# A two-layer metaformer block on one core: the load of x by tokens moved behind the spectral loads, ScalarE's copies ahead of the next part, and a narrower subtraction of the taps

## The chip, the core and the metric

The kernel runs on one core of a Trainium2 chip. The metric is the device time of one execution in microseconds (us). Five engines work side by side: TensorE (PE; its weight loads are listed as PEld), VectorE (DVE), ScalarE (ACT), GpSimd (POOL) and SyncE (SP), which here issues all data transfers. They meet only at semaphores: an instruction waits until a counter has reached a value, and its engine executes in program order, so everything behind a waiting instruction waits as well.

## The reference

The input x is 8 x 64 x 64 x 64 (batch, channels, height, width). Every step is a residual one:

```
x = x + spectral_conv(layernorm_channels(x))      # 32 x 32 kept modes, kernel looked up by f1^2 + f2^2
t = tokens(x);  t = t + moe(layernorm(t))         # 8 experts of 64 x 64, the best 2 of a softmax router
x = x + depthwise_conv_29x29(layernorm_channels(x))
t = tokens(x);  t = t + moe(layernorm(t))
```

## The kernel before, in words

**Stages.** The x that is held in SBUF has three layouts in turn. `xr` (x by rows) and `xb` (x by channels) are loaded first, in pieces; VectorE measures the layer norm's statistics on `xr` and TensorE takes the first Fourier transform from `xb`. `xr` lies in the region `X`. Once it has been measured, the same region takes x by tokens (`x_tok`, four transfers of 2 MB), onto which the result of the spectral convolution is added much later. The order of the work is written out by hand in every engine's program.

**The spectral product.** 136 complex matrices of 64 x 64 are read in eight blocks of 17 (`t` = 0 to 7, from `spec_pairs`). SyncE loads block `t` into one of three buffers; for `t` of 3 and more it first waits until VectorE has split block `t - 3` (`k_low`). ScalarE (`row_high`, L1172) takes the high half of each block, VectorE (`row_low`, L747) the low half, and TensorE multiplies (L1492, about 1000 small matmuls, straight-line code without a loop). Then follow transposes (L1558), the inverse transforms (L1570 and L1707), and VectorE adds the result to X (L1069), which waits for `x_tok`.

**SyncE's order before.** In the loop over the blocks, at `t` = 2, it waits until all of `xr` has been measured (`piece_measured`) and then issues the four transfers of `x_tok`; the loads of blocks 3 to 7 and the weights of the experts come behind them in the same queue.

**The expert stage.** It runs once for each layer, over 8 chunks of 32 token tiles. A chunk has 16 pairs `p`. For pair `p` TensorE multiplies two tiles with seven experts (L1605, L1606: `expert_pair`), VectorE multiplies the result with the gates (L904: `weigh_pair`), GpSimd adds the products (L571, L581), and TensorE sums four tiles in PSUM every second pair (L1616, L1619: `sum_quad`).

Beside it the same engines prepare the chunks ahead, in parts `(k, j)` of 8 tiles, four to a chunk. Each part goes through a chain of five steps:

1. ScalarE: `normalise` (8 activations, L1249, cut in two halves of 4) and `take_high` (L1261), which writes the high half in f16
2. VectorE: `low_parts` (L844), the low half. The next part's `normalise` waits for it, since both use one PSUM bank
3. TensorE: `turn_tokens` (L1583), 8 transposes into another single bank, which must have been copied out before
4. ScalarE: `copy_parts` (L1278, L1279), the copy out of that bank
5. TensorE: `route` (L1593, L1594), the router's logits; VectorE then computes the gates in 15 small steps (L866 to L892)

The first chunk of each layer is `start_chunk`, whose order stands in tables. At pair `p` ScalarE starts the first half of `normalise` by `START_NORMS = {1: (1, 2), 3: (1, 3), 5: (2, 0), 8: (2, 1), 12: (2, 2)}`, does the second half one pair later, and copies by `START_TURNS = {0: (1, 0), 3: (1, 1), 5: (1, 2), 7: (1, 3), 9: (2, 0), 13: (2, 1)}`. A first half and a copy fall on the same pair at 3 and at 5 only. TensorE turns by the same table, behind its `expert_pair(p)`; VectorE does `low_parts` at pairs 1, 3, 5, 7, 10 and 14.

**The taps.** The 29 x 29 taps of the depthwise convolution are split into high and low f16 halves within the first layer's start chunk: `taps_high` on ScalarE at pair 10 (L1316), `taps_low` on VectorE at pair 13 (L950). Both run over all 2412 columns of a padded row, in which the taps of a channel fill 29 rows of 29 at a pitch of 38; the rest is zero. `taps_low` works on partitions 64 to 127 only.

Of the kernel before, what the change touches and what calls it, by code (L numbers as in the profile page):

```python
# [15 lines left out]
B, C, H, W = 8, 64, 64, 64  # L16
# [6 lines left out]
NT = HB * WB * B  # L23
BO, BP, B2 = 2, 2, 2
BH, BQ = 2, 4
KS = 29
NE = 8
KRING = 3
PITCH = 38
# [4 lines left out]
CENTRE = 31 * PITCH + 23  # L34
TAP_SCALE = 256.0
# [32 lines left out]
def metaformer(nc, x_chan, x_rows, x_tok, spec_pairs, spec_last, dft, dft16, inv_h, inv_c, ident, ident16,  # L68
               experts0, experts1, rank, taps, out):
    ctx = ExitStack()  # L70
    with ctx:
# [11 lines left out]
        X = sb("X", NT * C)  # L83
# [63 lines left out]
        taps_f32 = R1[:, 5120:5120 + TAPS]  # L147
# [21 lines left out]
        x_in = sem("x_in")  # L169
# [189 lines left out]
        @block.sync  # L359
        def _(sp):  # L360
            def piece(i):
                return slice(i * PC, (i + 1) * PC)

            def unit(i):
                piece, g0, g1 = UNITS[i]
                return slice(piece * PC + g0 * C, piece * PC + g1 * C)

            def load_rows(i):
                sp.dma_start(X[:, unit(i)], x_rows[:, unit(i)]).then_inc(xr_in[i], 16)

            def load_channels(i):
                sp.dma_start(xb[:, unit(i)], x_chan[:, unit(i)]).then_inc(xb_in[i], 16)

            load_rows(0)
            sp.dma_start(dft_sb[:, :], dft).then_inc(dft_in, 16)
            sp.dma_start(rank_sb[:, :], rank).then_inc(rank_in, 16)
            load_channels(0)
            load_rows(1)
            load_channels(1)
            load_rows(2)  # L380
            load_rows(3)
            load_channels(2)
            load_rows(4)
            load_channels(3)
            load_channels(4)
            load_rows(5)
            load_channels(5)
            sp.dma_start(dft16_sb[:, :], dft16).then_inc(const_in, 16)
            lo, hi = BLOCKS

            for r, i in ((lo, 0), (hi, 1)):
                sp.dma_start(last_raw[r, 0:17, 0:64], spec_last[:, i]).then_inc(last_in, 16)
                sp.dma_start(last_raw[r, 0:17, 64:128], spec_last[:, 1 - i]).then_inc(last_in, 16)

                sp.dma_start(last_raw[r, 17, 0:64], spec_last[:, 1 - i, 16]).then_inc(last_in, 16)
                sp.dma_start(last_raw[r, 17, 64:128], spec_last[:, i, 16]).then_inc(last_in, 16)
            sp.dma_start(inv_h_sb[:, 0:64], inv_h).then_inc(const_in, 16)
            sp.dma_start(inv_c_sb[:, :], inv_c).then_inc(const_in, 16)
            sp.dma_start(ident_sb[:, :], ident).then_inc(const_in, 16)
            sp.dma_start(ident16_sb[:, :], ident16).then_inc(const_in, 16)  # L400
            for t in range(NSTEP):
                if t < 3:
                    sp.wait_ge(c_dft, 20 + 2 * t)
                else:
                    sp.wait_ge(k_low, 2 * (t - 2))
                for r in BLOCKS:
                    sp.dma_start(k_raw[t % 3][r], spec_pairs[:, PER_STEP * t:PER_STEP * t + PER_STEP, :]
                                 ).then_inc(k_in[t % 3], 16)
                if t == 2:

                    sp.wait_ge(piece_measured, len(UNITS))
                    for i in range(4):
                        n = NT * C // 4
                        sp.dma_start(X[:, i * n:(i + 1) * n], x_tok[:, i * n:(i + 1) * n]).then_inc(x_in, 16)

            wait_c_dft_low(sp, 32)
            sp.dma_start(raws_at[0], experts0).then_inc(raw_in, 16)

            sp.wait_ge(inv2, 32)
            for r in BLOCKS:  # L420
                sp.dma_start(taps_f32[r], taps).then_inc(taps_in, 16)
            sp.wait_ge(taps_step, TAPS_STEPS)
            for p in range(P):
                at = (WI - 1 - p // HI) * PITCH + HI - 1 - p % HI
                sp.wait_ge(y_used, 12 + 17 * p // 20)
                sp.dma_start(taps_dram[:, :, p, :].rearrange("s c n -> (s c) n"),
                             taps_16[:, at:at + WINDOW]).then_inc(taps_out, 16)
            sp.wait_ge(taps_out, P * 16)

            def load_bands(c, i):  # L430
                src = bass.AP(taps_dram[:, :, :, :].tensor, c * P * WINDOW,
                              [[WINDOW, P], [C * P * WINDOW, 2], [1, WINDOW]])
                sp.dma_start(bands[i], src).then_inc(bands_in[i], 16)

            sp.wait_ge(summed, NOCT * (NCHUNK - 1))
            load_bands(0, 0)
            sp.wait_ge(summed, NOCT * NCHUNK)
            for i in range(1, 4):
                load_bands(i, i)
            sp.dma_start(raws_at[1], experts1).then_inc(raw_in, 16)  # L440
            with sp.Fori(0, C // 4 - 1) as m:
                for i in range(4):
                    sp.wait_ge(blocks_ready, 4 * m + i + 1)
                    sp.wait_ge(low_blocks_ready, 4 * m + i + 1)
                    load_bands(4 * m + 4 + i, i)
            sp.wait_ge(conv_copied, C)

            def store(tile, tiles):
                at = slice(tile * C, (tile + tiles) * C)
                sp.dma_start(out[:, at], X[:, at]).then_inc(stored, 16)  # L450

            for i in range(2 * NCHUNK - 1):
                sp.wait_ge(sum_copied, NOCT * NCHUNK + (i + 1) * NOCT // 2)
                store(i * CT // 2, CT // 2)
            sp.wait_ge(sum_copied, 2 * NOCT * NCHUNK - 1)
            store(NT - 16, 8)
            sp.wait_ge(last_copied, 2)
            store(NT - 8, 4)
            sp.wait_ge(sum_copied, 2 * NOCT * NCHUNK)
            store(NT - 4, 4)  # L460
            sp.wait_ge(stored, (2 * NCHUNK + 2) * 16)
# [195 lines left out]
        def _(dve):  # L657
# [288 lines left out]
            def taps_low():  # L946

                dve.wait_ge(taps_step, 1)
                r = BLOCKS[1]
                dve.scalar_tensor_tensor(out=taps_16[r], in0=taps_f32[r], scalar=TAP_SCALE, in1=taps_16[r],  # L950
                                         op0=ALU.mult, op1=ALU.subtract).then_inc(taps_step, 1)

            def plane_stats(lo, hi):
# [167 lines left out]
        def _(act):  # L1121
# [117 lines left out]
            def normalise(layer, k, q, j, tiles=range(8)):  # L1239

                n = layer * NCHUNK + k
                if 0 in tiles:
                    if j == 0:
                        act.wait_ge(tok_step, (n + 1) * TOK_STEPS)
                    if layer or j or k:
                        act.wait_ge(tok_low, n * 4 + j)
                for t in tiles:
                    at = 8 * j + t
                    last = act.activation(xn_psum[:, t * C:(t + 1) * C], X[:, bass.ds(k * CT * C + at * C, C)],  # L1249
                                          ACT.Identity, bias=small[2 * q][:, at:at + 1],  # L1250
                                          scale=small[2 * q + 1][:, at:at + 1])
                if 7 not in tiles:
                    return
                last.then_inc(tok_normed, 1)
                if layer or k:
                    act.wait_ge(across, n * 4 + j - 3)
                act.wait_ge(tok_normed, n * 4 + j + 1 - 4 * layer)
                take_high(j, xn_psum)
# [59 lines left out]
            def start_chunk(layer):  # L1318
                for p in range(NPAIR):
                    if p % 4 == COPY_AT and p >= 4 * SUM_LAG:  # L1320
                        copy_sum(layer, 0, p // 4 - SUM_LAG)
                    if p in START_NORMS:
                        k, j = START_NORMS[p]
                        normalise(layer, k, k % 2, j, range(0, 4))
                    if p - 1 in START_NORMS:
                        k, j = START_NORMS[p - 1]
                        normalise(layer, k, k % 2, j, range(4, 8))
                    if p in START_TURNS:
                        k, j = START_TURNS[p]
                        copy_parts(layer, k, k % 2, j)  # L1330
                    if p == 2:
                        root_seed(layer, 2, 0)
                    if not layer and p == 10:
                        taps_high()
                    if p == START_EXP:
                        exp_second(layer, 1)
                    if p == ROOT_AT:
                        root_seed(layer, 3, 1)
# [453 lines left out]
```

## Time and profile before

| | us |
|---|---|
| median of 3 runs (lowest, highest) | 957.55 (956.13, 961.07) |
| the profiled execution | 955.84 |
| its span | 954.1 |
| VectorE busy in the span | 774.4 |
| GpSimd busy in the span | 567.5 |
| ScalarE busy in the span | 506.9 |

The page gives TensorE as busy for 850.6 us, with a mean granted clock of 0.936 of full speed. The stretches of the span are: Fourier transforms to 82 us, spectral product to 115 us, inverse transforms to 186 us, first expert stage to about 449 us, depthwise convolution to about 684 us, second expert stage to the end. The chain that ended last passes from engine to engine; what is taken from it shortens the span, as long as no other wait takes its place.

### The profile page before, as it was taken

The page shows a single profiled execution, that of the slowest core. Times are in us where ns is not written, and L with a number is a line of the kernel's source. Part 1 is how long each engine was busy: PE and PEld are TensorE (multiplying, and loading weights), DVE is VectorE, ACT ScalarE, POOL GpSimd, SP SyncE. Part 2 cuts the span into 40 slices and gives each one's busy share as a digit, 9 for nine tenths or more (in the row PEclk, how much of TensorE's full clock was granted, in tenths as well). Part 3 has the DMA queues.
Part 4 walks back from the last instruction along what each step waited for, and adds up shares of the span by engine and source line. Part 5 has one row for each costly group of instructions (what it writes and reads, how often), then busy time and mean ns, then how long its engine had stood idle before and what let it go on. Part 6 is the DMA issues. An engine that isn't in the chain of part 4 may idle for free.

```text
span 954.1 us, 24392 instructions
## 1 busy us (share of the span) xinstructions
PE 850.6 (89%) x9482; PEld 699.1 (73%) x9482; DVE 774.4 (81%) x1421; ACT 506.9 (53%) x1051; POOL 567.5 (59%) x504
## 2 busy tenths in 40 slices
PE   6997888677999998996899999999658999999998
PEld 6996877645676666654899999999635666667665
DVE  5768698888999989999787677774787999998884
ACT  2467485786667766211444444444168676676511
POOL 3780203157798887796654334330216888889888
PEclk9997577988999999999899999999959999999999
DMA  9997100103777776683787877888000010101101
GB/s 377 355 294 258 50 1 2 40 15 153 281 311 300 301 300 274 280 323 122 265 282 253 286 264 259 274 275 264 13 1 13 33 46 24 45 24 45 46 40 49
DMA packets 48291, 163.09 MB, mean 171 GB/s; under 512 B 9424, under 2 KB 9936, under 8 KB 46032
## 3 DMA queue, kind: packets, MB, share of 16 engines
q1 hardware_dynamic: 48208, 161.96, 46.7%
q8 instruction: 55, 0.90, 0.4%
q14 instruction: 28, 0.23, 0.1%
HBM read 93.46 MB, written 68.49 MB: 170 GB/s over the span
## 4 chain that ended last, share of the span: by engine, by line
PE 50%; DVE 31%; POOL 6%; issue 5%; DMA 3%; ACT 3%; SPq 1%; POOLq 0%; DVEq 0%; ACTq 0%
PE pair L1692 23%; DVE R L904 11%; PE pair L1619 5%; PE pair L1605 5%; PE pair L1606 4%; DMA X<-x_rows 3%; PE pair L1616 3%; DVE R L844 3%; PE pair L1492 3%; POOL R L571 3%; DVE R L660 2%; PE pair L1583 2%; DVE R L833 2%; DVE work L660 2%; ACT pair L1249 1%
## 5 line engine op out<-in xcount | busy, mean ns | idle before, releaser
L904 DVE TENSOR_TENSOR R<-pair,R 128x896 f32<-128x896 f32 x256 | 275.1, 1082 | 41.8 <-PE pair L1606 40.6
L571 POOL TENSOR_TENSOR R<-R 128x768 f32<-128x768 f32 x128 | 231.9, 1812 | 85.8 <-DVE R L904 76.7
L1692 PE MATMUL pair<-R 128*128 (+4 forms) x2880 | 226.8, 242 | 9.8 <-DVE R L982 9.2
L1692 PEld LDWEIGHTS pair<-R 128*128 128x128 f16 x2880 | 223.9, 98 | 12.9 <-issue 10.5
L1249 ACT ACTIVATE pair<-X,work 128x64 f32<-128x64 f32 x480 | 166.7, 394 | 97.1 <-DVE R L844 94.6
L1605 PE MATMUL pair<-work,R 128*128 128x448 f16 x512 | 185.0, 361 | 22.4 <-DVE R L904 20.9
L1606 PE MATMUL pair<-work,R 128*128 128x448 f16 x512 | 184.4, 360 | 0.0
L581 POOL TENSOR_TENSOR R<-R 128x512 f32<-128x512 f32 x128 | 164.9, 1288 | 10.0
L997 DVE COPY R<-R 128x1152 f32<-128x1152 f32 x64 | 93.1, 1455 | 64.9 <-PE pair L1692 64.3
L1367 ACT COPY R<-R 128x1152 f32<-128x1152 f32 x64 | 81.9, 1282 | 117.4 <-PE pair L1692 117.4
L1619 PE MATMUL pair<-R,ident_sb 128*128 128x256 f32 x496 | 128.4, 381 | 0.0
L623 POOL TENSOR_TENSOR R<-X,work 128x1024 f32<-128x1024 f32 x15 | 43.9, 2929 | 103.5 <-DVE R L988 90.4
L1605 PEld LDWEIGHTS pair<-work,R 128*128 128x128 f16 x512 | 50.7, 99 | 73.7 <-DVE R L904 42.3
L1619 PEld LDWEIGHTS pair<-R,ident_sb 128*128 128x128 f32 x496 | 95.0, 191 | 13.1
L660 DVE BATCH_NORM_STATS2 work<-X 128x6 f32<-128x128 f32 x384 | 84.9, 282 | 14.4 <-DMA X<-x_rows 14.4
L1616 PE MATMUL pair<-X,inv_h_sb 128*128 128x256 f32 x248 | 79.7, 403 | 0.0
L1291 ACT ACTIVATE X<-pair 128x512 f32<-128x512 f32 x62 | 36.0, 580 | 73.8 <-PE pair L1625 73.8
L1606 PEld LDWEIGHTS pair<-work,R 128*128 128x128 f16 x512 | 50.9, 99 | 30.7 <-issue 2.0
L1583 PE MATMUL pair<-ident_sb,R 128*128 128x128 f16 x512 | 42.9, 232 | 33.9 <-DVE R L844 27.1
L1583 PEld LDWEIGHTS pair<-ident_sb,R 128*128 128x128 f16 x512 | 36.1, 104 | 48.2 <-DVE R L844 30.4
L1453 PE MATMUL pair<-dft_sb,R 128*128 128x68 f32 x256 | 56.1, 422 | 9.1 <-DMA R<-x_chan 9.1
L1453 PEld LDWEIGHTS pair<-dft_sb,R 128*128 128x128 f32 x256 | 55.2, 333 | 9.3 <-issue 8.9
(137 smaller groups left out, 1292.7 us busy)
## 6 DMA issues: line engine op xcount, KB each, us to landing
taps_halves<-R SPq DMA_DIRECT2D x128, 458.5 KB, 3.3
R<-taps_halves SPq DMA_DIRECT2D x64, 917.0 KB, 4.8
X<-x_tok SPq DMA_DIRECT2D x4, 2048.0 KB, 17.8
out<-X SPq DMA_DIRECT2D x15, 512.0 KB, 2.6
R<-spec_pairs SPq DMA_DIRECT2D x16, 272.0 KB, 5.4
X<-x_rows SPq DMA_DIRECT2D x4, 1024.0 KB, 10.6
R<-x_chan SPq DMA_DIRECT2D x4, 1024.0 KB, 13.7
X<-x_rows SPq DMA_DIRECT2D x2, 2048.0 KB, 27.3
```

The source lines that it names most:

```text
L571: pool.tensor_tensor(pr[:, :, 192:384], pr[:, :, 0:192], pr[:, :, 192:384], ALU.add).then_inc(half_ready, 1)
L581: pool.tensor_tensor(w, pr[:, :, 192:320], pr[:, :, 320:448], ALU.add).then_inc(quarter_ready, 1)
L660: return dve.bn_stats(out_.rearrange("p t k -> p (t k)"), rows.rearrange("p t c -> p c t"))
L904: dve.tensor_tensor(pr.rearrange("p t (e c) -> p t e c", c=C), pair[p % 2][:, :].rearrange("p (t e c) -> p t e c", t=2, c=C)[:, :, 0:NE - ...
L1249: last = act.activation(xn_psum[:, t * C:(t + 1) * C], X[:, bass.ds(k * CT * C + at * C, C)], ACT.Identity, bias=small[2 * q][:, at:at + 1 ...
L1453: mm = pe.matmul(c_dft_bank(n)[:, j * 68:(j + 1) * 68], xb[:, (4 * n + j) * P:(4 * n + j + 1) * P], dft_sb[:, :], start=True, stop=True)
L1583: mm = pe.transpose(out_[:, t * P:(t + 1) * P], parts[j][:, t * P:(t + 1) * P], ident16_sb[:, :])
L1605: pe.matmul(dst, u[q][:, t * P:(t + 1) * P], wa[:, 0:EW], start=True, stop=False)
L1606: mm = pe.matmul(dst, vh[q][:, t * P:(t + 1) * P], wb[:, 0:EW], start=False, stop=True)
L1616: pe.matmul(bank[7][:, 256 * half:256 * (half + 1)], ident_scaled, X[:, bass.ds((k * NQUAD + g) * 256, 256)], start=True, stop=False)
L1619: pe.matmul(bank[7][:, 256 * half:256 * (half + 1)], ident_sb[:, :], w[:, :, j, :], start=False, stop=False)
L1692: mm = pe.matmul(acc[:, y0:y1, x0:x1, :], blocks[i % 2][:, ks, 2 - y, 1 - x, :], src[:, y0 + y:y1 + y, x0 + x:x1 + x, :], start=(ks == 0 a ...
```

## The change

SyncE issues `x_tok` behind all eight blocks and behind the first layer's expert weights. In the start chunk of both layers ScalarE does `copy_parts` ahead of the first half of `normalise` where both fall on one pair. `taps_low` runs over the 29 rows of 29 columns that hold taps.

```diff
@@ block.sync
                     sp.dma_start(k_raw[t % 3][r], spec_pairs[:, PER_STEP * t:PER_STEP * t + PER_STEP, :]
                                  ).then_inc(k_in[t % 3], 16)
-                if t == 2:
-
-                    sp.wait_ge(piece_measured, len(UNITS))
-                    for i in range(4):
-                        n = NT * C // 4
-                        sp.dma_start(X[:, i * n:(i + 1) * n], x_tok[:, i * n:(i + 1) * n]).then_inc(x_in, 16)
 
             wait_c_dft_low(sp, 32)
             sp.dma_start(raws_at[0], experts0).then_inc(raw_in, 16)
+            sp.wait_ge(piece_measured, len(UNITS))
+            for i in range(4):
+                n = NT * C // 4
+                sp.dma_start(X[:, i * n:(i + 1) * n], x_tok[:, i * n:(i + 1) * n]).then_inc(x_in, 16)
@@ taps_low
-                dve.scalar_tensor_tensor(out=taps_16[r], in0=taps_f32[r], scalar=TAP_SCALE, in1=taps_16[r],
+                first = CENTRE - KS // 2 * (PITCH + 1)
+                f32, f16_ = (m[r, first:first + KS * PITCH].rearrange("p (x y) -> p x y", y=PITCH)[:, :, 0:KS]
+                             for m in (taps_f32, taps_16))
+                dve.scalar_tensor_tensor(out=f16_, in0=f32, scalar=TAP_SCALE, in1=f16_,
                                          op0=ALU.mult, op1=ALU.subtract).then_inc(taps_step, 1)
@@ start_chunk on ScalarE
-                    if p in START_NORMS:
-                        k, j = START_NORMS[p]
-                        normalise(layer, k, k % 2, j, range(0, 4))
                     if p - 1 in START_NORMS:
                         k, j = START_NORMS[p - 1]
                         normalise(layer, k, k % 2, j, range(4, 8))
                     if p in START_TURNS:
                         k, j = START_TURNS[p]
                         copy_parts(layer, k, k % 2, j)
+                    if p in START_NORMS:
+                        k, j = START_NORMS[p]
+                        normalise(layer, k, k % 2, j, range(0, 4))
```

## Rows read from the trace of the kernel before

**Rows 1.** The page's part 4: the chain that ended last, by engine.

```profile
PE 50%; DVE 31%; POOL 6%; issue 5%; DMA 3%; ACT 3%; SPq 1%; POOLq 0%; DVEq 0%; ACTq 0%
```

**Rows 2.** Timeline, PE, spectral product: start, us, engine, line, operation, count, idle before.

```profile
82.50 3.88 PE L1492 MATMUL pair<-R 128*128 128x16 f16 x143 [1.50 <-DVE R L729]
89.23 3.56 PE L1492 MATMUL pair<-R 128*128 128x16 f16 x128 [2.85 <-issue]
92.96 3.56 PE L1492 MATMUL pair<-R 128*128 128x16 f16 x128 [0.18 <-issue]
96.97 3.58 PE L1492 MATMUL pair<-R 128*128 128x16 f16 x128 [0.44 <-issue]
101.25 13.49 PE L1492 MATMUL pair<-R 128*128 128x16 f16 x487 [0.70 <-issue]
```

**Rows 3.** DMA queues from 72.7 to 74.5 us: packets, MB, share.

```profile
q8 instruction: 1, 0.02, 3.8%
```

**Rows 4.** DMA queues from 82.6 to 86.4 us, the only queue listed.

```profile
q1 hardware_dynamic: 213, 0.72, 86.5%
```

**Rows 5.** DMA queues from 86.4 to 88 us.

```profile
q8 instruction: 1, 0.02, 5.0%
```

**Rows 6.** Windows: stretch, us, busy by engine, PE clock, DMA share, GB/s.

```profile
60.00:80.00 20.00, 15.81 (x199) 14.99 (x197) 15.58 (x26) 14.96 (x26) 8.23 (x12) 1.00 1.02 413
231.00:237.70 6.70, 4.56 (x47) 3.49 (x48) 5.29 (x12) 3.95 (x10) 4.52 (x4) 0.50 0.99 385
```

**Rows 7.** Timeline of SP's queue, 0 to 220 us: DMA issues.

```profile
56.40 2.02 SPq L414 DMA_DIRECT2D X<-x_tok  x4
...
74.55 21.36 SPq L407 DMA_DIRECT2D R<-spec_pairs  x10
```

**Rows 8.** Timeline of all engines: VectorE's first addition to X.

```profile
151.68 0.69 DVE L1069 TENSOR_TENSOR X<-X,pair 128x512 f32<-128x512 f32 x1 [1.63 <-PE pair L1707]
```

**Rows 9.** Timeline of ACT, start chunk of the first layer.

```profile
201.75 1.40 ACT L1249 ACTIVATE pair<-X,work 128x64 f32<-128x64 f32 x4
203.09 0.57 ACT L1278 COPY R<-pair 128x512 f32<-128x512 f32 x1
...
206.93 1.40 ACT L1249 ACTIVATE pair<-X,work 128x64 f32<-128x64 f32 x4 [0.82 <-DVE R L844]
...
210.72 0.59 ACT L1261 CAST R<-pair 128x512 f16<-128x512 f32 x1
```

**Rows 10.** Timeline of PE, the same chunk: the transposes of part (1, 2).

```profile
204.28 0.61 PE L1583 MATMUL pair<-ident_sb,R 128*128 128x128 f16 x8 [2.35 <-ACT R L1279]
```

**Rows 11.** Timeline of DVE, first layer: pairs 6 and 10, taps, last gate, pair 2.

```profile
207.70 1.09 DVE L904 TENSOR_TENSOR R<-pair,R 128x896 f32<-128x896 f32 x1 [0.46 <-PE pair L1606]
...
216.86 1.09 DVE L904 TENSOR_TENSOR R<-pair,R 128x896 f32<-128x896 f32 x1 [0.70 <-PE pair L1606]
...
224.75 3.59 DVE L950 SCALAR_TENSOR_TENSOR R<-R 64x2412 f16<-64x2412 f32 x1
...
232.61 0.39 DVE L892 TENSOR_TENSOR R<-R,pair 128x224 f32<-128x224 f32 x1
...
239.61 1.09 DVE L904 TENSOR_TENSOR R<-pair,R 128x896 f32<-128x896 f32 x1 [2.47 <-PE pair L1606]
```

**Rows 12.** Timeline of ACT, start chunk of the second layer.

```profile
718.56 1.40 ACT L1249 ACTIVATE pair<-X,work 128x64 f32<-128x64 f32 x4
```

**Rows 13.** Timeline of PE, start chunk of the second layer: part (1, 2).

```profile
721.09 0.61 PE L1583 MATMUL pair<-ident_sb,R 128*128 128x128 f16 x8 [3.36 <-ACT R L1279]
```

**Rows 14.** Timeline of DVE, second layer: pairs 6 and 10, last gate, pair 2.

```profile
726.17 1.09 DVE L904 TENSOR_TENSOR R<-pair,R 128x896 f32<-128x896 f32 x1 [2.13 <-PE pair L1606]
...
734.12 1.09 DVE L904 TENSOR_TENSOR R<-pair,R 128x896 f32<-128x896 f32 x1 [0.70 <-PE pair L1606]
...
746.13 0.39 DVE L892 TENSOR_TENSOR R<-R,pair 128x224 f32<-128x224 f32 x1
...
751.23 1.09 DVE L904 TENSOR_TENSOR R<-pair,R 128x896 f32<-128x896 f32 x1 [1.34 <-PE pair L1606]
```

## The prediction

> **What bounds the kernel now.** I read the chain that ended last first. It is half TensorE and a third VectorE, with ScalarE and GpSimd together under a tenth [rows 1], so no engine is the limit throughout, and each edit must be weighed where it acts. I then read the timelines of three stretches: the spectral product, where the chain is TensorE's matmuls, and the start chunk of each expert stage, where it wanders between ScalarE, TensorE and VectorE. The last 50 us are GpSimd's additions, but these start when VectorE delivers, so what is gained earlier shifts them as a whole.
>
> **x by tokens behind the blocks.** The edit adds and removes nothing; it moves four transfers of 2 MB past ten block loads and one load of expert weights. Before, they are issued at 56.4 us and fill the DMA engines from 60 to 80 us at 413 GB/s [rows 6, 7]. The block loads that wait behind them could make ScalarE late, but ScalarE's split of block 3 must wait for TensorE's block 0 anyway, and the wait for the load that is left is 0.6 us and not on the chain. So the order of data is worth nothing here.
>
> What I do see is TensorE's idle time for "issue". The matmuls of L1492 come in groups: 143, then three times 128, then 487, with gaps of 2.85, 0.18, 0.44 and 0.70 us ahead of the later four [rows 2]. Each matmul has one weight load, so the groups are 256 instructions long, and the queue named "instruction" moves packets of 0.02 MB. I read the gaps as TensorE waiting for its own code. Going back 128 matmuls from the gap at 86.4 us, the block of code before it was entered at 82.9 us. The packet that should have started then is missing from 82.6 to 86.4 us, while other traffic holds 86.5% of the engines [rows 4], and appears behind 86.4 us [rows 5]. It came late because block 3, held up by `x_tok`, and block 4 then move together. Without `x_tok` ahead of it block 3 is in by 79 us, and only block 4 is in the way. The later groups met one such load each, at gaps of 0.18 to 0.70 us. I take 0.5 us for the gap: a gain of 2.85 - 0.5 = 2.3 us, bounds 0 (the gap stays) and 2.85 (it goes).
>
> Against this stands the new place. The block loads end at 95.9 us [rows 7], a little earlier then, and the expert weights follow; `x_tok` moves its 8 MB from about 95 to 115 us, by the 20 us that it takes now [rows 6]. TensorE enters four or five blocks of code in that time. How does a fetch fare beside `x_tok`? One row shows it: a block entered at 73.0 us got its packet within the stretch to 74.5 us [rows 3], in the middle of the full load. A group of 487 matmuls in 13.49 us without a gap [rows 2] is 27.7 ns each, or 3.55 us for a block, and the fetches just keep pace. I charge 0.1 us for each of five: 0.5 us. Bounds: nothing, and 5 times the 2.35 us by which the first gap exceeds an ordinary one, 12 us. I take the low end, since the row at 73 us is the one under this very load. X is not needed before 151.7 us [rows 8], 35 us behind its arrival, so nobody waits for it; if that cover were gone, VectorE's additions would wait. GpSimd's own wait for `x_in` moves from a time when it idles to another. This edit: 2.3 - 0.5 = 1.8 us gained, bounds -12 and +2.9.
>
> The Trainium skill (Runtime: NRT & Kernel Launch, Instruction fetch mechanics) says that code is streamed in blocks of 256 instructions, one being fetched while the other executes, and that crossing into a new block is mostly hidden. The block length agrees with the groups of 128 matmuls and 128 loads; that it is hidden does not agree with the gaps of 0.18 to 2.85 us [rows 2]. By that rule the gap would have another cause, this edit would be worth nothing, and the sum below would be 8.8 us instead of 10.6.
>
> **Copies ahead of the next part.** This acts at pairs 3 and 5 of both start chunks. First layer, pair 3: ScalarE is free at 201.7 us, runs four activations to 203.1 us, and only then copies part (1, 1), which TensorE had turned by 200.4 us [rows 9]. TensorE stands for 2.35 us until this copy's end before it turns part (1, 2) [rows 10]. With the copy first, 0.57 and 0.57 us overlapping to 1.0, TensorE goes on at 202.8 instead of 204.3 us. The total of ScalarE's work up to `take_high` of (1, 3) is the same, so VectorE's low half of it does not come later (206.2 us). Pair 5: ScalarE idles 0.82 us for that low half and then normalises from 206.93 us [rows 9]. With the copy of (1, 2) first, turned by 203.5 us now, 1.0 us of copying fills the idle time; `normalise` starts at 207.0, and `take_high` of (2, 0) moves from 210.7 to 209.75 us.
>
> Followed through: VectorE's pair 6 moves from 207.7 to 207.2 (TensorE no longer late), its low half of (2, 0) from 211.3 to 210.35, pair 8 from 212.9 to 211.4, pair 9 to 212.8, the two first gate steps to 214.65. TensorE can turn (2, 0) once (1, 3) is copied at 211.2, and has pair 10 ready 2.6 to 3.3 us later, at most 214.6. Pair 10 starts at 214.7 instead of 216.86 us [rows 11]: 2.15 us. From there VectorE has no idle time to the end of the chunk, and the gain stays.
>
> Second layer: TensorE waits 3.36 us for the same copy [rows 13], ScalarE starts with the activations at 718.56 us [rows 12], and pair 6 comes at 726.17 us with 2.13 us of idle time for TensorE [rows 14]. With the copy first, TensorE turns at 719.7, pair 6 is ready at 723.0 and VectorE takes it at 724.0, behind its low half (unchanged at 722.95). `take_high` of (2, 0) is done at 727.2 instead of 728.1, pair 8 goes from 730.15 to 728.25, TensorE turns (2, 0) at 728.35 behind the copy of (1, 3), and pair 10 starts at 731.7 instead of 734.12 [rows 14]: 2.4 us. Both: 4.55 us. Bounds: a loss of 1.0 us for each pair and layer, if the copies only postpone the chain of `normalise` (-4), and a gain of both of TensorE's waits, 2.35 + 3.36 = 5.7 us.
>
> **The taps.** 29 x 29 = 841 elements instead of 2412. At the rate of the row, 3.59 us / 2412 = 1.49 ns each [rows 11], that is 1.25 us: 2.34 us less on VectorE, which runs without idle time from pair 10 to the last gate. `taps_high` is ready long before. Pairs 14 and 15 are waiting from TensorE. Bounds: 0 if a strided row costs as much as the full one, 3.1 us if only a small fixed part is left.
>
> **The clock behind the taps.** While VectorE works on the taps TensorE has nothing to do, and from 231.0 to 237.7 us its granted clock is 0.50, the 1.2 GHz level [rows 6]. Just there it is late: pair 2 of the next chunk comes at 239.61 us after 2.47 us of idle time [rows 11]. From the end of the last gate step (233.0) to pair 2 it is 6.6 us. In the second layer, with no taps and at full clock, the same way takes 751.23 - 746.52 = 4.7 us [rows 14]. With the taps shorter TensorE's stop before is about 0.6 instead of 2.9 us, as in the second layer, and I expect its clock to stay up: 1.9 us, bounds 0 and 2.5 (the whole idle time).
>
> **Sum.** 1.8 + 4.55 + 2.34 + 1.9 = 10.6 us. The profiled execution took 955.84 us and lies 1.7 us under the median of the runs, 957.55. 957.55 - 10.6 = 947.0 us.
>
> **The rivals.**
> - *The code fetch and the clock give nothing.* The first gap has another cause or block 4 alone holds the packet up as long, and the clock drops as before, since TensorE also idles 2.7 us for the last gate. For it: a single block load already makes gaps up to 0.70 us. Against it: the second layer. Left are 4.55 + 2.34: 950.7 us.
> - *The copies gain half.* VectorE's low half of (1, 3) is not earlier by either order, and at pair 8 another wait (GpSimd's sums for the four product buffers) may come up. For it: the chain is short of slack everywhere. Against it: GpSimd idles 1.4 to 2 us ahead of each addition here. Left are 2.3 + 2.34 and one of the other two terms: 951.0 to 952.9 us, say 952.
> - *Slower: the code fetch starves beside `x_tok`.* Place: the spectral product from 95 to 115 us, where TensorE runs through a block of code in 3.55 us and is itself the chain. Price: if each of five fetches comes late as the one at 82.9 us did, 5 x 2.65 = 13 us; if none is served until the 20 us of transfer are over, about 18 us. For it: the packet that is missing for 3.6 us in rows 4. Against it: rows 3. Then it is 957.55 - 11.1 + 13 = 959.5, or up to 965 us. It turns the sum above 2.2 us a fetch.
> - *The first edit does nothing and the rest works* lies within the range of the forecast, at 948.8 us.
>
> **How the numbers follow.** Forecast, with 944 to 950 us as its own range: 0.52. First rival 0.18, second 0.14, slower rival 0.07, and 0.09 for more than I sum up (stretches at the lower clock may fall at other places once the stages start earlier, and where TensorE is the chain that is worth 1 to 2 us either way). A measurement of this kernel can tell 0.5% (4.8 us) from no change, so faster means below 952.8 us. That holds for the forecast, the first rival, most of the second and the better case: 0.79. Within 0.5%: 0.15, slower 0.06. The range from 942 to 955 us leaves out the slower rival and tails.
>
> **What would show it.** In the profile after: the gap ahead of the second group of L1492 under 1 us, and no gap over 0.5 us from 95 to 115 us; TensorE's wait for L1279 ahead of part (1, 2) shorter by 1.4 us in both layers, and pair 10 earlier by about 2 us against the stage's start; L950 at 1.25 us; a clock of 1.0 throughout the first 15 us of the first layer's second chunk. The prediction is wrong if gaps named "issue" of 2 us stand in the spectral product, or if `normalise` of (2, 0) comes later than before.

## The result, and the profile after

The changed kernel takes 961.39 us (median of 20 runs, 959.64 to 962.69) against 957.33 us (20 runs, 954.24 to 961.07): ratio 1.0039, 95% interval 1.0031 to 1.0048. It is slower by 4 us where 10 us less were forecast. The profiled execution took 961.60 us, with a span of 959.8. Of all runs below one stands apart, 2939.71 us among the 12 of the copies alone, and its ratio leaves it out.

I lay the starts of VectorE's 256 `weigh_pair` beside each other, after minus before. They show where the time comes and goes:

| place | before, us | after minus before, us |
|---|---|---|
| first layer, pair 0 | 194.87 | +8.50 |
| pair 6 | 207.70 | +7.81 |
| pair 10 | 216.86 | +7.35 |
| pair 14 (behind the taps) | 228.37 | +5.70 |
| next chunk, pair 2 | 239.61 | +5.93 |
| second layer, pair 0 | 710.12 | +5.86 |
| pair 6 | 726.17 | +3.49 |
| pair 10 | 734.12 | +4.24 |
| next chunk, pair 2 | 751.23 | +5.74 |

So 8.5 us are lost ahead of the expert stage. The first layer's start chunk gains 1.15 us by the copies (pair 0 to pair 10) and 1.65 us by the taps (pair 10 to pair 14), the second layer's 1.6 us by the copies; and 0.2 and 1.5 us go again behind the two start chunks.

The loss stands in TensorE's timeline of the spectral product (start, us, line, count, idle before), which answers to [rows 2]:

```profile
82.26 3.90 PE L1493 MATMUL pair<-R 128*128 128x16 f16 x143 [1.70 <-DVE R L727]
87.06 3.56 PE L1493 MATMUL pair<-R 128*128 128x16 f16 x128 [0.89 <-issue]
91.07 3.56 PE L1493 MATMUL pair<-R 128*128 128x16 f16 x128 [0.45 <-issue]
96.44 3.58 PE L1493 MATMUL pair<-R 128*128 128x16 f16 x128 [1.81 <-issue]
102.64 3.79 PE L1493 MATMUL pair<-R 128*128 128x16 f16 x128 [2.62 <-issue]
109.12 3.79 PE L1493 MATMUL pair<-R 64*64 64x16 f16 x128 [2.69 <-issue]
115.60 3.58 PE L1493 MATMUL pair<-R 128*128 128x16 f16 x128 [2.69 <-issue]
120.98 2.91 PE L1493 MATMUL pair<-R 128*128 128x16 f16 x103 [1.80 <-issue]
```

Now every group of 128 matmuls has a gap before it, and the gaps sum to 12.95 us instead of 4.17. The first shrank from 2.85 to 0.89 us; where `x_tok` moves, the last four are 1.8 to 2.7 us wide. The clock does not tell the two kernels apart here: in every stretch of 4 us from 84 us to the end of the product it is 0.50 to 0.52, the 1.2 GHz level, in both. SyncE's queue, which answers to [rows 7], and one window of the stretch (as in [rows 6]: clock, DMA share, GB/s at the end):

```profile
95.21 2.28 SPq L415 DMA_DIRECT2D X<-x_tok  x4
```

```profile
104.00:108.00 4.00, 2.43 (x91) 2.33 (x87) 2.57 (x2) 1.49 (x2) 0.00 (x0) 0.50 1.00 422
```

The block of code that TensorE entered at 102.64 us has its fetch missing from 103 to 106.6 us, while data holds the DMA engines, and present right behind:

```profile
q1 hardware_dynamic: 110, 1.54, 100.6%
```

```profile
q1 hardware_dynamic: 36, 0.59, 100.7%
q8 instruction: 1, 0.02, 4.8%
```

This is the same picture as in [rows 4, 5], once for each block of code. The start chunk, VectorE's timeline after, answers to [rows 11]: pairs 6 and 10, the taps, pair 2 of the next chunk.

```profile
215.51 1.07 DVE L902 TENSOR_TENSOR R<-pair,R 128x896 f32<-128x896 f32 x1
...
224.21 1.09 DVE L902 TENSOR_TENSOR R<-pair,R 128x896 f32<-128x896 f32 x1 [1.19 <-PE pair L1607]
...
232.09 1.95 DVE L951 SCALAR_TENSOR_TENSOR R<-R 64x841 f16<-64x841 f32 x1
...
245.54 1.09 DVE L902 TENSOR_TENSOR R<-pair,R 128x896 f32<-128x896 f32 x1 [2.69 <-PE pair L1607]
```

TensorE's timeline, answering to [rows 10, 13]. Its wait for the copy fell from 2.35 to 0.36 us and from 3.36 to 1.87 us, but a new one stands five pairs later, for ScalarE's first copy of a sum:

```profile
211.31 0.61 PE L1584 MATMUL pair<-ident_sb,R 128*128 128x128 f16 x8 [0.36 <-ACT R L1280]
...
221.64 0.67 PE L1617 MATMUL pair<-X,inv_h_sb 128*128 128x256 f32 x2 [0.83 <-ACT X L1292]
...
725.47 0.61 PE L1584 MATMUL pair<-ident_sb,R 128*128 128x128 f16 x8 [1.87 <-ACT R L1280]
...
735.80 0.67 PE L1617 MATMUL pair<-X,inv_h_sb 128*128 128x256 f32 x2 [0.82 <-ACT X L1292]
```

Two windows of the kernel after at the lower clock: behind the first layer's start chunk, as before, and behind the second layer's, where it was at full clock before; pair 2 answers to the last of [rows 14].

```profile
237.10:243.90 6.80, 5.05 (x49) 3.83 (x50) 4.90 (x12) 3.55 (x9) 4.83 (x3) 0.50 1.00 382
...
752.50:755.90 3.40, 3.40 (x30) 2.68 (x28) 1.63 (x5) 1.06 (x2) 3.32 (x3) 0.50 0.00 0
```

```profile
756.97 1.09 DVE L902 TENSOR_TENSOR R<-pair,R 128x896 f32<-128x896 f32 x1 [2.84 <-PE pair L1607]
```

### The profile page after: what moved, and what is told of

Its sections match the earlier page's. It is cut to its first block, busy times and chain, and to the rows that moved or that the text cites. A ratio compares the mean times of both kernels' runs of the same rounds, so it can differ in the third digit from the quotient of the medians.

```text
span 959.8 us, 24392 instructions
## 1 busy us (share of the span) xinstructions
PE 850.5 (89%) x9482; PEld 698.0 (73%) x9482; DVE 771.9 (80%) x1421; ACT 506.1 (53%) x1051; POOL 566.4 (59%) x504
## 4 chain that ended last, share of the span: by engine, by line
PE 48%; DVE 30%; issue 7%; POOL 6%; ACT 5%; DMA 3%; SPq 1%; POOLq 0%; DVEq 0%; ACTq 0%
PE pair L1693 23%; DVE R L902 11%; PE pair L1620 5%; PE pair L1606 4%; PE pair L1607 4%; DMA X<-x_rows 3%; PE pair L1617 3%; PE pair L1493 3%; POOL R L569 3%; DVE R L842 3%; DVE R L658 2%; ACT pair L1250 2%; DVE work L658 2%; DVE R L831 2%; PE pair L1584 2%
## 5 line engine op out<-in xcount | busy, mean ns | idle before, releaser
L569 POOL TENSOR_TENSOR R<-R 128x768 f32<-128x768 f32 x128 | 231.9, 1812 | 85.1 <-DVE R L902 74.1
## 6 DMA issues: line engine op xcount, KB each, us to landing
X<-x_rows SPq DMA_DIRECT2D x4, 1024.0 KB, 11.2
```

What stands on the lines that cost most here:

```text
L569: pool.tensor_tensor(pr[:, :, 192:384], pr[:, :, 0:192], pr[:, :, 192:384], ALU.add).then_inc(half_ready, 1)
```

## The experiments

**x_tok alone behind the blocks** (the first hunk of the diff, nothing else).

> x_tok moved behind the blocks, nothing else changed. Theory 1 (TensorE's code fetches starve beside x_tok): gaps named issue of 2.6 to 2.7 us between groups of 128 matmuls as in the changed kernel, the first expert stage starts 8.5 us later than in the kernel before, and the time is 957.3 + 8 = 965 to 966 us. Theory 2 (the load in its new place is harmless, the loss of 4 us comes from the new orders of ScalarE and VectorE): 955 to 957.5 us, gaps under 1 us.

965.12 us against 958.05, ratio 1.0077 (1.0062 to 1.0092). TensorE's groups from 97 us on:

```profile
97.13 3.59 PE L1490 MATMUL pair<-R 128*128 128x16 f16 x128 [1.79 <-issue]
104.42 3.79 PE L1490 MATMUL pair<-R 128*128 128x16 f16 x128 [3.71 <-issue]
110.89 3.80 PE L1490 MATMUL pair<-R 64*64 64x16 f16 x128 [2.68 <-issue]
116.82 3.58 PE L1490 MATMUL pair<-R 128*128 128x16 f16 x128 [2.13 <-issue]
121.64 2.91 PE L1490 MATMUL pair<-R 128*128 128x16 f16 x103 [1.24 <-issue]
```

The whole loss, and more, is in this one edit: +7 us.

**The copies alone** (the third hunk).

> ScalarE's copies ahead of the first half of normalise, nothing else changed. Theory 1: pair 10 comes 1.2 us earlier in the first layer and 1.6 us earlier in the second, less than the 2.15 and 2.4 forecast, since TensorE now waits 0.8 us for ScalarE's first copy of a sum; 954.5 us if no stretch at the lower clock moves against it, 956 if one does as in the second layer of the changed kernel (1.5 us). Theory 2 (this order is the loss): 959 us or more.

956.25 us, ratio 0.9986 (0.9976 to 0.9996). TensorE waits 0.8 us for the copy of the first sum here too. Pair 10 gained 1.15 us and 1.6 us against the start of its stage, and 0.5 us went again behind the first start chunk and 1.6 us behind the second, where a stretch at the lower clock stands (747.5 to 750.7 us).

**The taps alone** (the second hunk).

> taps_low over 29 rows of 29 columns, nothing else changed. Theory 1: the instruction takes 1.95 us instead of 3.59 as in the changed kernel, and the time falls by 1.6 us to 955.7 us; the clock behind it still drops to 0.50. Theory 2 (TensorE's shorter stop keeps its clock up): 3.5 us less, 953.8 us.

956.26 us, ratio 0.9980 (0.9968 to 0.9991). The instruction took 1.95 us, and the clock behind it still fell, for 6.8 us. So the 1.65 us come in and the clock's 1.9 us don't. The profiled executions of these two kernels, which have `x_tok` at its old place, show gaps of 5.39 and 7.15 us in all in the spectral product, where that of the kernel before had 4.17: executions differ in this by some microseconds.

**x_tok behind the spectral product**, with both other edits.

```diff
             sp.wait_ge(piece_measured, len(UNITS))
+            sp.wait_ge(mixed, NMIX)
             for i in range(4):
```

> The changed kernel, but x_tok is issued only when TensorE has finished the whole spectral product, so that it moves from about 115 to 137 us beside the transposes and inverse transforms, where TensorE waits for VectorE anyway. Theory 1 (a transfer beside code that runs without a pause): the gaps of 2.6 us are gone, the first gap stays near the 0.9 us of the changed kernel, the product ends 1.5 to 2.5 us earlier than before, and the time is 957.3 - 2 - 2.8 = 952 to 954 us. Theory 2 (x_tok costs the same wherever its 20 us are put): 959 to 962 us.

952.43 us, ratio 0.9947 (0.9933 to 0.9960): 5 us faster than before and 9 us faster than the changed kernel, by one wait. TensorE's groups, as above:

```profile
87.04 3.56 PE L1494 MATMUL pair<-R 128*128 128x16 f16 x128 [0.79 <-issue]
91.33 3.56 PE L1494 MATMUL pair<-R 128*128 128x16 f16 x128 [0.72 <-issue]
95.88 3.58 PE L1494 MATMUL pair<-R 128*128 128x16 f16 x128 [0.99 <-issue]
100.16 11.05 PE L1494 MATMUL pair<-R 128*128 128x16 f16 x384 [0.70 <-issue]
111.37 2.92 PE L1494 MATMUL pair<-R 128*128 128x16 f16 x103 [0.15 <-issue]
```

The gaps sum to 3.35 us. The same 8 MB now move from 114 to 137 us at 366 GB/s beside the transposes and inverse transforms, and cost nothing that can be seen. TensorE's transposes behind the product, in the kernel before and in this one:

```profile
116.43 11.17 PE L1558 MATMUL pair<-ident_sb,R 128*102 128x128 f16 x136 [1.69 <-DVE R L811]
```

```profile
115.98 10.63 PE L1560 MATMUL pair<-ident_sb,R 128*102 128x128 f16 x136 [1.69 <-DVE R L810]
```

The fetch of code is late here too: its packet starts at 120.38 us, 6.1 us behind the end of the product, where in the kernel before it started at 117.61 us, 2.9 us behind it. But no gap named "issue" follows from 116 to 150 us. These transposes take 78 ns each, so a block of 128 of them lasts 10 us and not 3.56, and a fetch that comes 3 us late is still in time. So it is the length of the block that hides the fetch, and not TensorE's waiting for VectorE, as I had expected: within these transposes it waits for nobody. This is read from the two profiles; no run of its own tests it.

**Smaller rows.** The changed kernel with 16 transfers of 4 KB rows for 4 of 16 KB.

```diff
-            for i in range(4):
-                n = NT * C // 4
+            for i in range(16):
+                n = NT * C // 16
                 sp.dma_start(X[:, i * n:(i + 1) * n], x_tok[:, i * n:(i + 1) * n]).then_inc(x_in, 16)
```

> The changed kernel, with x_tok in 16 transfers of 512 KB (rows of 4 KB) in place of 4 of 2 MB (rows of 16 KB), at the same place. Theory 1a (a fetch of code waits for a number of packets that are queued ahead of it on its DMA engine, each of 16 KB and 0.61 us): smaller packets shorten the wait, the gaps of 2.7 us shrink to 1.0 us or less, and the time is 955 to 957 us. Theory 1b (it waits for its share of a loaded engine, whatever the packets): gaps of 2.7 us, 961 us.

961.04 us, ratio 1.0040 (1.0026 to 1.0053), with gaps of 3.17, 2.41, 2.41 and 2.62 us under the load. The size of the rows makes no difference; theory 1a has fallen. The Trainium skill (DMA: Bandwidth & Descriptors, Queues, rings and completion order) says that a DMA engine takes turns between queues packet by packet. By that rule packets a quarter as long should have made the wait for a turn shorter. The packets did become shorter (4 KB and 0.16 us each by their records, for 16 KB and 0.61 us), and this run does not agree: its wide gaps of 2.41 to 3.17 us are no narrower than the 1.80 to 2.69 us of the changed kernel.

**Half of x_tok behind the product** (two transfers at the new place, then `sp.wait_ge(mixed, NMIX)`, then two).

> The changed kernel, with two of the four transfers of x_tok behind the blocks and two behind the spectral product. Theory 1 (each fetch beside the transfer costs 2.7 us): the stretch under load is half as long, two of the four gaps of 2.7 us remain, and the time lies midway between the changed kernel and the one with x_tok behind the product: 956 to 957.5 us. Theory 2 (any piece of x_tok in the product makes the same delay, as through a single late load): 960 us or more.

957.01 us, ratio 0.9987 (0.9976 to 0.9999), midway between 961.4 and 952.4. Two of the wide gaps are left, 3.17 and 2.41 us, and then it runs on:

```profile
102.78 3.79 PE L1495 MATMUL pair<-R 128*128 128x16 f16 x128 [3.17 <-issue]
108.98 7.32 PE L1495 MATMUL pair<-R 64*64 64x16 f16 x256 [2.41 <-issue]
116.73 2.91 PE L1495 MATMUL pair<-R 128*128 128x16 f16 x103 [0.43 <-issue]
```

The price goes with the time under load: one late fetch for each block of code that is entered in it.

**Spare traffic in the kernel before.**

```diff
             sp.dma_start(raws_at[0], experts0).then_inc(raw_in, 16)
+            for i in range(4):
+                n = NT * C // 4
+                sp.dma_start(spare_dram[:, i * n:(i + 1) * n], x_tok[:, i * n:(i + 1) * n]).then_inc(spare_out, 16)
```

> The kernel before, with x_tok at its old place, and behind the expert weights four more transfers of 2 MB from the input to a spare DRAM region that nobody reads or waits for until the end. Theory 1 (traffic alone delays the fetches): gaps of 2 us and more between groups of 128 matmuls from 96 us on, and 963 to 967 us. Theory 2 (the loss comes from x_tok writing SBUF or from somebody waiting for it): no such gaps, 957 to 959 us.

970.73 us, ratio 1.0138 (1.0122 to 1.0154). Nobody reads this region, X is where it was, and the gaps are there: 1.52, 2.41, 3.23 and 3.45 us.

```profile
102.81 3.79 PE L1498 MATMUL pair<-R 128*128 128x16 f16 x128 [1.52 <-issue]
109.01 3.79 PE L1498 MATMUL pair<-R 64*64 64x16 f16 x128 [2.41 <-issue]
116.04 3.58 PE L1498 MATMUL pair<-R 128*128 128x16 f16 x128 [3.23 <-issue]
123.07 2.91 PE L1498 MATMUL pair<-R 128*128 128x16 f16 x103 [3.45 <-issue]
```

Traffic alone does it. It cost 13 us, more than expected: this kernel has both the late first gap of the kernel before (3.08 us) and the new ones, and the transfer to DRAM lasted to about 125 us instead of 118, at 307 to 344 GB/s from 108 us on instead of 430, so that the last block, too, met a fetch of full lateness (3.45 us instead of 1.80). Pair 0 comes 11.2 us later than in the kernel before; another 1.2 us goes at the lower clock behind the second start chunk.

**The copy of the first sum ahead of the next part.** `x_tok` behind the product, and in the start chunks:

```diff
+                    if p == 8:
+                        copy_sum(layer, 0, 0)
-                    if p % 4 == COPY_AT and p >= 4 * SUM_LAG:
+                    if p % 4 == COPY_AT and p > 4 * SUM_LAG + COPY_AT:
                         copy_sum(layer, 0, p // 4 - SUM_LAG)
```

> The changed kernel with x_tok behind the product, and in both start chunks ScalarE's first copy of a sum ahead of the first half of normalise at pair 8 in place of pair 9. Theory 1 (the reordered copies gain 1.0 and 0.8 us less than forecast because TensorE now waits 0.8 us in each layer for this copy): TensorE's wait for L1292's counterpart goes, pair 10 comes 0.5 to 0.8 us earlier in each layer, and the time is 951 to 952 us. Theory 2 (the low half of part (2, 0) sets pair 10, not TensorE): unchanged, 952.4 us.

949.68 us, ratio 0.9912 (0.9898 to 0.9926); a second measurement gave 950.03 us against 956.85, ratio 0.9932 (0.9910 to 0.9954).

> The kernel with x_tok behind the product and the sum copy at pair 8 once more, beside the one with taps_low behind pair 14, so that their difference of 0.9 us is read on one chip. Theory 1: 949 to 951 us and 0.9 us above the other. Theory 2: the same as the other.

In the first layer TensorE's `sum_quad` ahead of pair 10 no longer waits, and pair 10 gained 2.1 us against pair 0, as forecast for the change. A wait of 1.0 us for the second copy of a sum stands ahead of pair 14 instead; there VectorE has the taps to do, and pair 14 is not later for it. In the second layer the gain is 1.7 us in the first profiled execution, which fell back to the lower clock for 3.4 us within the start chunk (717.0 to 720.3 us), and 2.6 us in the second, which did not. Against the kernel without this edit (1.15 and 1.6 us) that is 1.0 us a layer where nothing disturbs it, and theory 1's mechanism holds. The size by the times is not settled: set against 0.9947 the two ratios give 3.4 and 1.4 us, and the second interval overlaps that of the kernel without the edit (0.9933 to 0.9960).

**The taps behind pair 14** (`p == 13` to `p == 14` for `taps_low`, on top of the last kernel).

> The kernel with x_tok behind the product and the sum copy at pair 8, with taps_low behind pair 14 in place of pair 13, where GpSimd runs only its small Newton steps. Theory 1 (taps_low stood 1.0 us of its 1.95 us behind GpSimd's addition of 1.81 us that had begun before it; its own 841 elements take 0.9 us): the instruction takes 0.9 to 1.1 us, GpSimd's addition behind it is back at 1.27 us, and the time falls by 0.9 us, to 948.8 us. Theory 2 (a strided row of 29 costs 2.3 ns an element wherever it runs): 1.95 us again, 949.7 us.

949.39 us against 950.03, ratio 0.9921 (0.9900 to 0.9941) beside 0.9932. The mechanism of theory 1 shows, its gain does not: the intervals overlap almost wholly. VectorE's timeline and GpSimd's small step beside it, which takes 0.24 us elsewhere:

```profile
223.49 1.09 DVE L903 TENSOR_TENSOR R<-pair,R 128x896 f32<-128x896 f32 x1 [0.66 <-PE pair L1610]
226.00 1.03 DVE L952 SCALAR_TENSOR_TENSOR R<-R 64x841 f16<-64x841 f32 x1
```

```profile
226.08 1.06 POOL L551 TENSOR_TENSOR work<-work,rank_sb 128x32 f32<-128x32 f32 x1
```

The taps take 1.03 us, and GpSimd's second addition, now ahead of them, is back at 1.27 us; but pair 14, reached earlier, waits 0.66 us for TensorE; at the next chunk the two kernels are 0.1 us apart.

## Why the prediction was wrong

**The code fetch: the mechanism was right, and the row that was to price it was misread.** The cause of the gaps was named correctly, and so was what would happen in the worst case: the rival that starves "beside `x_tok`" is what the chip did. The step that failed is "a block entered at 73.0 us got its packet within the stretch to 74.5 us", from which I charged 0.1 us a fetch. The packet in [rows 3] is real; the 73.0 us was not read but counted back over some 13 us of timeline, through instructions and records whose number is not exact. The kernel after shows the error. There TensorE has the same code up to this place and the same pace (its groups of L1471 start at 70.25 and 72.48 us, those of the kernel before at 70.49 and 72.72), and from 70.5 to 72.4 us, with no `x_tok` moving, its queue has

```profile
q8 instruction: 1, 0.02, 3.5%
```

Its packet starts at 71.3 us by the packet's own record, that of the kernel before at 73.9. So the block was entered before 71.3 us, and the fetch beside `x_tok` was 2.4 us late, 2.64 less the 0.24 us by which TensorE is ahead in the kernel after. The other profiles agree: the packet starts at 73.9 to 74.1 us in the four kernels with `x_tok` at its old place, and at 71.2 to 72.0 us in the eight profiles of the others. No gap followed there because TensorE, waiting for VectorE, did not reach the next block before about 82.9 us, by the count in the prediction. The row that I took as evidence for harmlessness showed the price: the 2.35 us of my upper bound. I had both figures in the same text and took the low end by the row "under this very load". The last four gaps of the kernel after sum to 9.80 us; the same four blocks have 0.85 us with `x_tok` behind the product, and 1.95 to 2.22 us in the three profiles of the later kernels with that order. All gaps together are 8.8 us more than in the kernel before, and pair 0 comes 8.5 us later.

The spare traffic shows that the load alone suffices, the half transfer that it goes by the time under load, and the wait on `mixed` that the same late fetch costs nothing beside the transposes, where a block of code lasts 10 us. The Trainium skill (Runtime: NRT & Kernel Launch, Instruction fetch mechanics) calls the crossing mostly hidden; in the profiled executions here it is not: even with `x_tok` behind the product gaps of 0.15 to 2.07 us stand ahead of most of its blocks.

**The first gap: right.** Forecast 2.3 us less, measured 1.96 less (2.85 to 0.89), and 0.75 to 1.11 us in the other kernels without `x_tok` ahead of block 3, against 2.45 to 3.28 us with it.

**The copies: right in direction, about half in size.** Forecast 4.55 us, measured 2.8. TensorE did go on earlier, pair 6 came as computed (0.7 us earlier against pair 0 instead of 0.5; 2.4 in the second layer instead of 2.2), and so did pair 8. I then followed `normalise` and `turn_tokens` up to pair 10 but left out ScalarE's `copy_sum`, which stands at pair 9 behind the first half of `normalise` (2, 1), and for which `sum_quad` at pair 10 waits. With pair 10 reached earlier it became the last: 1.15 instead of 2.15 us, 1.6 instead of 2.4. Put one pair earlier, it gives the first layer's forecast value.

**The taps: the term was mis-sized.** Forecast 1.25 us for 841 elements at 1.49 ns, measured 1.95. The rate was taken from a row in which VectorE had stood still. In the kernel before, GpSimd's addition of 1.81 us began at 224.00 us and ended at 225.81; the taps "start" at 224.75 and end at 228.34, which is 225.81 plus 2412 elements at 1.05 ns. In the kernel after GpSimd's addition runs from 231.34 to 233.14 us, and the taps end at 234.04: 0.9 us, or 1.07 ns an element, behind it. The waiting is the same in both; what falls away is 1571 elements at 1.05 ns, 1.65 us (measured 1.64). GpSimd's next addition, held up from its usual 1.27 to 3.57 us before, takes 1.94 us after. The Trainium skill (SBUF — State Buffer, Who interferes with whom) says that a VectorE instruction with two inputs in SBUF and a GpSimd instruction that reads SBUF exclude each other for their whole length, whichever began first winning. Both directions agree with these rows, and so does the run with the taps at pair 14 (1.03 us).

**The clock behind the taps: wrong.** I blamed TensorE's stop of 2.94 us during the taps. With the stop shortened to 1.22 us (0.6 had been forecast) the clock fell to 1.2 GHz at the same place for 6.8 us, in the kernel after and with the taps alone; pair 2 waited 2.69 us. In three of the later profiles it fell for 3.4 us there, one of them with a stop of only 0.26 us. And the second start chunk, which I had held up as the undisturbed case, fell too once the stage began at another time: 1.5 us lost at pair 2 in the kernel after and 1.6 us with the copies alone, nothing in one profiled execution of the kernel with the sum copy at pair 8 and 1.6 us in another of the same code. Which of the short stops there lowers the clock is still open.

**The sum.** Forecast 1.8 + 4.55 + 2.34 + 1.9. By the profiles after and before: -8.5 + 2.8 + 1.64, then -0.2 and -1.5 behind the start chunks, 5.8 us slower. By the medians it is 4.1 us, since the profiled execution of before was one of the quicker ones (955.84 us against a median of 957.33); its gaps in the product, 4.17 us, are the shortest of the four profiles with `x_tok` at its old place.

**The rivals.** The slower rival, given 0.07, holds the measured time in its 959.5 to 965 us, but not by its terms, so its number is in part luck. It took off 11.1 us for the rest of the change, where the first gap, the copies, the taps and the clock brought 4.7 (2.0 + 2.8 + 1.6 - 1.7); and it charged 13 us or more for the fetches, where the gaps behind the first grew by 10.7. Its 2.65 us a fetch is neither of the figures in rows and text that it could rest on, 2.85 and 2.35. In the second rival one of the other two terms gives 951.0 or 951.1 us; its 952.9 takes neither.

## What to carry to other kernels

Straight-line code that TensorE runs through at 28 ns a matmul has no room for a late fetch. A large transfer belongs beside a stage in which 256 instructions last longer than the fetch is late (10 us in the transposes here), and not only where its data is needed late enough. A gap named "issue" every 256 instructions is the sign to look for. A duration that serves as a rate must be checked for a neighbour that was running when the instruction began, and a moment that is counted back through a timeline must be checked against a second kernel before a price hangs on it.

## What the runs showed of the hardware that was not expected

A fetch of 16 KB of TensorE's code, beside transfers that fill the DMA engines, came too late for a block of 3.56 us of work: of 18 gaps under that load, in five kernels, 14 are 2.4 to 3.7 us wide, alike for rows of 16 KB and of 4 KB, and for a target in SBUF or in DRAM. The same 8 MB transfer so cost 9 us in one place (961.4 us against 952.4) and nothing that a profile shows 20 us later. Of the 12 us between the changed kernel and the best version, 949.4 to 950.0 us, 9 are that place.
